# Another steady order on the five engines of a pipelined scan, MoE and FFN kernel

## What is computed

```python
delta = softplus(x @ Wd + bd);  Bm = x @ WB + bB;  Cm = x @ WC + bC;  A = -exp(A_log)
# for each token t and state s
h = clip(exp(min(delta * A, 2)) * h + clip(delta * B, -2, 2) * x, -100, 100)
y = sum_s(h * C) + x * D_param
routing = softmax(y @ Wr + br);  e = argmax(routing)
moe = max(routing) * (silu(y @ up_w[e] + up_b[e]) @ down_w[e] + down_b[e])
x1 = layernorm(x + layernorm(y + moe) * ln_w + ln_b)
out = layernorm(x1 + (silu(x1 @ gate) * (x1 @ up)) @ down)
```

## Time and profile before

| | |
|---|---|
| median of 3 runs | 902.92 us (893.5 to 906.85) |
| time of the profiled execution | 904.75 us |
| its span | 902.9 us |
| VectorE busy | 726.7 us (80% of the span) |
| TensorE busy, matmuls | 661.3 us (73%) |
| GpSimd busy | 559.5 us (62%) |
| ScalarE busy | 516.4 us (57%) |
| mean granted clock of TensorE | 0.845 of its full 2.4 GHz |

### The profile page before, as it was taken

One profiled execution on the slowest core, in us unless ns is written; L12 is line 12 of the kernel. 1 busy time (PEld: TensorE's weight loads), 2 busy tenths in 40 slices (PEclk: granted clock), 3 DMA queues, 4 the chain that ended last, 5 costly groups with the idle time before them and its releaser, 6 DMA issues.

```text
span 902.9 us, 14264 instructions
## 1 busy us (share of the span) xinstructions
PE 661.3 (73%) x4264; PEld 535.5 (59%) x4322; DVE 726.7 (80%) x1458; ACT 516.4 (57%) x972; POOL 559.5 (62%) x452
## 2 busy tenths in 40 slices
PE   3365667877789768986988669986897489728856
PEld 1153445755588547864777548854786368717725
DVE  4699997789998999889979999799989995543152
ACT  5443164766576746775777538675776247425513
POOL 1357558658865876488757876589658835762051
PEclk8587676997899869997999679987998699959968
DMA  3333435685358544765557535863585347434410
GB/s 103 126 131 101 148 128 154 241 262 178 121 191 252 198 148 158 221 201 169 190 191 238 188 96 192 237 221 120 188 257 167 121 149 228 151 126 126 138 36 24
DMA packets 82088, 149.32 MB, mean 165 GB/s; under 512 B 9404, under 2 KB 51144, under 8 KB 81992
## 3 DMA queue, kind: packets, MB, share of 16 engines
q1 hardware_dynamic: 69192, 135.13, 46.6%
q0 software_dynamic: 4096, 8.40, 2.9%
q10 hardware_dynamic: 8704, 4.72, 1.8%
HBM read 132.80 MB, written 15.40 MB: 164 GB/s over the span
## 4 chain that ended last, share of the span: by engine, by line
DVE 32%; PE 21%; issue 19%; POOL 12%; ACT 8%; DMA 6%; SPq 1%; DVEq 1%; ACTq 0%; POOLq 0%
DVE state L1234 8%; DVE state L1248 6%; POOL prod L1280 4%; DVE psB L1229 4%; PE psT L711 4%; PE psU L697 4%; PE psY L567 3%; DMA weights<-in_w_pack 3%; DVE moe L1153 2%; DVE attn L1201 2%; DVE bst L1171 2%; POOL chosen_out L1309 2%; ACT decay L823 2%; POOL rows_in L1301 2%; PE psB L561 2%
## 5 line engine op out<-in xcount | busy, mean ns | idle before, releaser
L1280 POOL TENSOR_TENSOR prod<-state,c_wide 128x1024 f32<-128x1024 f32 x128 | 301.6, 2363 | 100.9 <-DVE state L1248 62.2
L1229 DVE TENSOR_TENSOR psB<-dx,psB 128x512 f32<-128x512 f32 x256 | 167.2, 684 | 24.8 <-PE psB L561 15.3
L823 ACT ACTIVATE decay<-delta,a_sb 128x1024 f32<-128x1024 f32 x128 | 140.4, 1141 | 61.0 <-DVE state L1248 59.5
L561 PE MATMUL psB<-parts,sel 128*128 128x512 bf16 x199 | 88.6, 448 | 115.8 <-DVE state L1248 58.6
L1248 DVE TENSOR_TENSOR_SCAN state<-decay,state,psB 128x512 f32<-128x512 f32 x128 | 163.2, 1275 | 8.5 <-issue 0.2
L567 PE MATMUL psY<-ident,prod 128*128 128x128 f32 x1024 | 161.9, 314 | 2.7 <-POOL prod L1280 1.1
L1234 DVE TENSOR_TENSOR_SCAN state<-decay,psB 128x512 f32<-128x512 f32 x128 | 155.0, 1211 | 0.0
L567 PEld LDWEIGHTS psY<-ident,prod 128*128 128x128 f32 x1024 | 146.5, 166 | 11.5 <-issue 5.4
L864 ACT ACTIVATE hid<-psU,weights 128x128 f32<-128x128 f32 x352 | 100.5, 369 | 60.6 <-PE psU L697 56.5
L561 PEld LDWEIGHTS psB<-parts,sel 128*128 128x128 bf16 x256 | 27.3, 107 | 160.5 <-DVE state L1234 94.4
L697 PE MATMUL psU<-yT_sorted,weights 128*128 128x128 f32 x704 | 99.5, 287 | 17.3 <-DMA weights<-in_w_pack 10.7
(11 more groups left out here) (163 smaller groups left out, 1116.2 us busy)
## 6 DMA issues: line engine op xcount, KB each, us to landing
c_wide<-c_rows SPq DMA_DIRECT2D x128, 512.0 KB, 5.1
weights<-in_w_pack SPq DMA_DIRECT2D x88, 514.0 KB, 4.3
xT_sb<-in_xT SPq DMA_DIRECT2D x8, 512.0 KB, 4.4
y_sorted<-rows_in SPq DMA_DIRECT2D x16, 256.0 KB, 3.2
rows_out<-result SPq DMA_DIRECT2D x16, 256.0 KB, 5.1
xt<-in_x SPq DMA_DIRECT2D x8, 512.0 KB, 5.1
out<-x ACTq DMA_DIRECT2D x16, 256.0 KB, 2.4
y_sorted<-rows_in SPq DMA_DIRECT2D x8, 192.0 KB, 4.4
```

The lines of the kernel that those rows point to most:

```text
L561: pe.matmul(tokens(psB, c, h), sel[:, s, :], parts[:, c.n % 2, h * HALF:h * HALF + c.hw], start=True, stop=True).then_inc(b_ready, 1)
L823: nc.scalar.activation(decay[:, g % NDECAY, w], delta[:, n % 2, w], ACT.Exp, scale=a_sb[:, s:s + 1]).then_inc(decay_ready, 1)
L1229: v.tensor_tensor(tokens(psB, c, h), dx[:, n % 2, h * HALF:h * HALF + c.hw], tokens(psB, c, h), ALU.mult).then_inc(inp_ready, 1)
L1280: g_.tensor_tensor(prod[:, g % NPROD, w], state[:, g % NSTATE, w], c_wide[:, g % NC, w], ALU.mult).then_inc(prod_ready, 1)
```

## The change

Only the tables change: PE_ORDER, ACT_ORDER, DVE_ORDER, POOL_ORDER and SP_ORDER, and three of the ends (PE_LAST, POOL_LAST, SP_LAST). The same tasks are run, each once per chunk, with the same instructions, buffers and waits; also the numbers of chunks by which they run ahead are shifted, since the tables now begin elsewhere in the loop. The diff has 160 lines of such entries, of which a few show the form:

```diff
 PE_ORDER = [
-    (-2, "spread", 15, 0), (-2, "spread", 15, 1), (-3, "down", 8), (-2, "add", 12), (-3, "up", 10),
...
+    (-4, "ff_part", 0, 0), (-3, "warm"), (-4, "ff_part", 0, 1), (-1, "b_spread", 0), (-2, "add", 8),
...
 POOL_ORDER = [
-    (-3, "prod", 14), (-3, "prod", 15), (-2, "prod", 0), (-4, "gather", 0), (-4, "gather", 1), (-4, "gather", 2),
...
+    (-4, "scatter", 1), (-3, "prod", 3), (-5, "gather", 6), (-5, "rstd", 0, 0), (-4, "scatter", 2),
+    (-4, "scatter", 3), (-4, "scatter", 4), (-3, "prod", 4), (-5, "rstd", 0, 1), (-3, "prod", 5), (-5, "gather", 7),
...
```

125 lines of the change are left out of this document (61 added, 64 removed), and 7 rows, old and new, of the table SP_ORDER.

## The result

The changed kernel takes 871.18 us in the median (869.45 to 876.24), against 902.86 before (893.5 to 906.85). The ratio on record, formed from the executions and not from these medians, is 0.968, 95% interval 0.960 to 0.976; two more executions of the changed kernel took 868.30 and 878.62 us and are not in its median. Forecast were 869 us in a range of 850 to 898, and a faster kernel with a chance of 0.66.

What follows compares the result with a forecast made beforehand. VectorE sets the pace. A steady chunk is 61.7 + 15.3 + 14.4 = 91.4 us against 97.2: −29 over five, −5 for outer iterations, −2 in the tail, so 904.75 − 36 = 869 us, range 850 to 898.

Steps and rivals of the forecast that it cites:

- Blocked steps: In (a), VectorE steps held beside GpSimd products: mean 6.1 us per chunk before, 1.3 taken as left.
- Start of a chunk: Fewer VectorE waits around the first scan: (a) shorter by 0.9 or 0.5 us in the two chunks, (c) by 0.6.
- (c): Stretch from bound 1 to the next chunk's first scan; forecast 14.4 us, from 15.0.
- dx: VectorE step of 1.21 us, moved out of (a) into the wait before bound 1, where it costs nothing.
- (a): Stretch from a chunk's first scan to bound 0; forecast 61.7 us, from 70.8 and 64.6 in the two chunks read.
- The chain to bound 0: In (a): TensorE's later b_spread 0 plus 0.8 us for table loads gives 61.7 us, above VectorE's 61.3 and 60.7.
- (b): Stretch from bound 0 to bound 1; forecast 15.3 us, from 15.2 and 14.8; wait before bound 1 falls to 2.8.
- Outer parts: Iterations on either side of the five steady ones −5 us together, the tail −2, start of the program nothing.
- rival 1: Combine 1 in (a) still meets products 6 and 7: 4.3 us per chunk, 894 us; chance 0.20.
- Rival 2: The chain to bound 0 is longer, through weights 2 and table loads: +2.4 us on average, 882 us; chance 0.10.
- Rival 3: VectorE about 1 us behind GpSimd in every chunk, four steps held, 11.8 us: 925 us; chance 0.08.
- Rival 4: Nothing is held and the chain stays hidden: 89.1 us per chunk, 854 us; chance 0.06.

Runs made afterwards that it cites:

- the run with three tables alone: The kernel before with the new order tables of TensorE, ScalarE and SyncE only, VectorE and GpSimd keeping the old: 930.2 us, ratio 1.033.

## Why the prediction was right

**VectorE bounds the kernel, through held steps: right.** Held time is what parts the long steady chunks from the short ones. VectorE's busy time, in which it counts, makes 10.7 of the 18.0 us that the five lost, and the shorter wait before bound 1 another 5.7. The runs with VectorE later and with the old start moved as a held step says, by 5 us a chunk for 0.6 to 0.7 us of shift.

**Blocked steps: right for the steps named, one place was overlooked.** Affine 0, combine 1 and centre 1 are clear in all steady chunks, and affine 1 meets the end of product 9 for 0.3 to 0.8 us, where 1.3 were charged. (The 6.1 us per chunk are the mean of the two chunks read; counted alike, the five have 5.3.) But the prediction priced four wide steps only. The change had put all five first gathers ahead of product 1 and router_shift a scan earlier; both stood in the text ahead of the prediction, and the prediction does not ask what the router's small steps, with both operands in SBUF, meet then. In three of five chunks they met product 1, and combine 0 product 3: 5.0 us each, 15 of the 29 forecast for these five chunks in the profiled execution (−18.0 measured).

**Start of a chunk: right in size, and worth more than its size.** 0.6 was forecast for (c), and putting the edits back gave 0.7. What it does to the phase was in the argument only as the reason to choose the good one.

**dx: too small.** It left (a) and cost nothing behind it; what it saves is up to 2.4 us, since it would be held at its old place with the new order.

**The chain to bound 0: the step that failed.** "TensorE decides: (a) is 61.7" is not so. The chain was worked out with TensorE's old start of b_spread 0, 57.5 us, as if that were its own, but TensorE's list is full of spreads that wait for VectorE, and so it came earlier as VectorE did. VectorE's own sum, 60.7 to 61.3, was the one measured, 60.9 to 61.5. The size of the error was 0.4 us; with the chain shortened, nothing was gained. The 0.8 us charged for the two table loads are not seen in (a) either, though the loads are there: ScalarE's busy time rose from 326.0 to 339.9 us in the five chunks, 2.8 each. The sign that went with this step, a wait before bound 0, did not show.

**(b) and (c): right.** 15.1 to 15.3 against 15.3, 14.1 to 14.4 against 14.4, and the wait before bound 1 2.5 to 2.7 against 2.8.

**Outer parts: mis-sized both ways.** The first, second and eighth chunks gave 10.9 us instead of 5. In the second, a conversion of the experts' biases was held for a whole product before (line 983, 2.37 us; 0.21 after), and VectorE's waits for spreads fell from 7.2 to 5.3 us and those before the bounds from 3.8 to 1.9; these were not looked at. The tail gave nothing instead of 2: up 3's wait for weights went, but VectorE waited 23.4 us for gathers there instead of 17.5. The start of the program, put at nothing, gave +0.2; the reason given, a table load of less than 1 us, does not fit the 1.28 of the earlier trace rows.

**The rivals.** Combine 1 (rival 1) was held in no steady chunk; in the one shown it was clear by 1.35 us, and gather 7 had landed 2.5 us after its issue, where 3.5 was the limit worked out; product 6 began 5.7 us after that issue, not 5.0. Rival 2 did not show: there was no wait at bound 0, and TensorE's matmuls waited for no weights in the five chunks (4.7 us before). Rival 3, the bad phase in every chunk, is what the run with three tables alone is. Rival 4 came nearest in the chunks of 90.2 us.

The sum came out near the median since the errors partly cancelled: against the forecast the profiled execution lost 11 us in the steady chunks and 2 in the tail and won 6 in the outer chunks, and four of the five other executions are 4 to 8 us shorter than it, one 2.4 longer. The size of the forecast was thus in part luck; that of a chunk without held steps was not.

## What to carry to other kernels

Where two engines lock each other out, an order is good or bad by a phase of half a microsecond: list every step that can be held, the 0.2-us ones too, and for each the distance to the neighbour's next long instruction, before and after. A wait ahead of such a place is worth a multiple of itself. Here the tables worked together or not at all: half of the reordering said nothing about the whole. When a chain on another engine seems to decide, look first whether it only follows the engine it is compared with. And before a late step is put down to the order, look at the granted clock of the stretch ahead of it.

## What the runs showed that was not expected

A VectorE step of 0.19 us with two operands in SBUF took up to 3.06 us, a whole product and more, although it was due 0.64 us ahead of the recorded start of the product (473.79 against 474.43). In the Trainium skill ("SBUF — State Buffer", "Who interferes with whom") the one that issues first has the ports for its whole instruction. The traces agree on the whole instruction. On who is first, recorded starts mislead in one case, which all the traces of this document show together, with combine, centre, affine, dx and the router's steps. Where GpSimd went from a gather or scatter straight to a product, 36 steps that began up to 0.71 us ahead of the product's recorded start stood until it, or a product right behind it, ended, and those that began 0.73 us or more ahead did not; between 0.67 and 0.71 both are found, and one step 0.17 ahead was not held. Where GpSimd had been idle for 0.3 us or more ahead of the product, none of 62 steps that began 0.14 to 0.71 us ahead was held. Combine 0's first piece in the long chunk of 367.39 is one of these; it began 0.17 us ahead of product 3, which had waited 0.69 us, and ran into it:

```profile
387.95 0.33 DVE L1152 SCALAR_TENSOR_TENSOR moe<-chosen_out,top_w,ytok 128x128 f32<-128x128 f32 x1
```

The gather itself does not hold them: no step that began in the last 0.7 us of a gather or scatter was held when another of these followed. That a product behind a gather is issued, and has the ports, while the gather's record still runs would fit all of this, and the rule; it is not shown.

The other way round, scatters are slowed beside delta (line 1043, two operands in SBUF, 1.2 us): in the changed kernel's five steady chunks the scatter that runs beside it took 1.59 to 1.61 us, where the median of all is 0.99.

The landing time of one transfer of 512 KB, 3.7 to 4.9 us within the steady chunks of one execution, went with the length of the chunk, 90 or 95 us, wherever product 1 and the start stand as in the change. What decides that landing time was not tried. In the two runs with gather 5 moved and z and bc in place, the one long chunk of each went with TensorE's granted clock instead.
